# First attention of a fused two-layer kernel: blanks written in pairs from an earlier half on, first batch's totals inverted sooner, maxima products repeated behind the break of a half

## The chip, the cores and the metric

The kernel runs on one NeuronCore of a Trainium2 chip. The metric is the device time of one execution in microseconds. An execution with the hardware profiler on gives the rows that are read here: which engine ran what, when, and at what granted TensorE clock. The engines are called PE (TensorE; PEld is its weight load), DVE (VectorE), ACT (ScalarE), POOL (GpSimd) and SP (SyncE, which here only issues transfers).

## What is computed

Four blocks on a batch of 4 sequences of 1024 tokens with 256 features, each followed by a residual sum and a layer norm: an attention with 16 heads of 16, a feed-forward of width 768, a causal attention with 8 heads, and a feed-forward of 16 experts. The change touches the first attention and its border with the feed-forward. That attention, with the reference's names:

```
q, k = apply_rope(layer_norm(q), layer_norm(k));  q = q * 16 ** -0.5
attn = softmax(einsum('bqhd,bkhd->bhqk', q, k), axis=-1)
out  = einsum('bhqk,bkhd->bqhd', attn, v).reshape(B, S, C)
x    = layernorm(x + out @ w_proj.T + b_proj)
```

## The kernel before

The first attention (`phase_attention0`) works through 16 **groups** of four heads of one batch, four groups to a batch. A group has 64 **units** (one tile of 128 keys, 512 queries, one head each) in two **halves** of 32. So there are 32 halves, counted by `u` from 0 to 31 (`TURNS`). Order on every engine is written out by hand, and the engines meet at semaphores only.

For each unit PE makes a **score** product (`score`, L867) into one of three PSUM banks, and ACT takes its exponential (L935). Score `s` waits for the exponential of three units before. PE goes in **bursts** of three units, and each burst may be followed by **value** products (`values`, L839), whose results lie `LAG` = 6 units and, in the first rounds of a half, up to `BREAK` = 3 more behind the scores. So at the start of each half there is a **break**: from unit 6 to unit 11 of the half no value products run. ACT also copies the finished half out there (`copy_out`, L928).

Softmax needs each query's maximum first. So with each unit PE also makes a **maxima** product (`max_product`, L814) for a unit `AHEAD` = 24 steps (48 units) later, into one of four banks, and DVE reduces it (`take`, L959). At the end of a half's 32 reductions DVE joins them (L968), POOL cuts the result in two parts (`cut_maxima`, L761 and L763), PE turns them (`turn_max`, L826; just before units 23 and 55 of a group, the **turn**), ACT copies them (L922), and SP moves them with four small transfers (`rows`, L695) into the queries' stack, where the first score of the next half waits for them. Both halves of a score or maxima product's pair use different rows of PE's array, so a score and a maxima product can run at the same time.

SP's queue holds, in this order in each group: the store of the last half of the group before (L702), the rows of its own second half, a **stack load** (L537 and L540: twelve transfers of 128 KB and one of 512 KB, for the group three later, up to group 12), the store of its first half, and the rows for the next group.

POOL's queue holds, in half `u`: `cut_maxima(u)`, fetches and preparation of weights (halves 6 to 17), and from half 18 (`FIRST_BLANKS`) five **blanks** a half (L792): transfers of about half a megabyte of zeros each, 32 in all, into two scratch arrays of the expert stage. Each blank waits for the landing of the one before. When all are out, POOL waits for the first tokens of the feed-forward (`xin`) and adds the bias to them (L798).

The exponentials' sums (**totals**) of the first three batches are read back at group 13 (`GROUPS - 3`), inverted by DVE when its last maximum is taken (L977), and written out as `shares` by SP in group 15. Then SP loads sums, shares and tokens of the first two blocks of the feed-forward (L487, L489, L502). The buffers for these are the stacks of groups 12 and 13. The fourth batch's totals are handled in the feed-forward.

Between the stages stands a barrier of all engines (L103). In the feed-forward (`phase_ffn0`) ACT's first function with a table of its own is the square root in `deviation` (L1336).

Of the kernel before, what the change touches and what calls it, by code (L numbers as in the profile page):

```python
# [14 lines left out]
P = 128  # L15
# [527 lines left out]
def phase_attention0(nc, d, keep, weights, stacks, shared):  # L543
# [68 lines left out]
    LAG, BREAK = 6, 3  # L612

# [36 lines left out]
    with ExitStack() as ctx:  # L650
# [28 lines left out]
        EARLY_TOKENS = (BATCH - 1) * SEQ  # L679
        totals = zero[:, 0:EARLY_TOKENS // shared.CUTS]  # L680
# [6 lines left out]
        def _(sp):  # L687
# [19 lines left out]
            for g in range(GROUPS):  # L707
# [9 lines left out]
                if g == GROUPS - 1:  # L717

                    sp.wait_ge(shares_made, 1)
                    sp.dma_start(shared.shares_of(d, slice(0, EARLY_TOKENS)), totals).then_inc(shares_out, 16)  # L720
                    sp.wait_ge(shares_out, 16)
                    sp.wait_ge(pv_done, (GROUPS - 2) * ROUNDS + RING // G0)
                    for n in range(2):
                        shared.load_sums(sp, d, n)
                        shared.load_tokens(sp, d, n)
# [3 lines left out]
                if g == 0:  # L729
                    stacks.load(sp, d, 0, 3)  # L730
                if g == GROUPS - 3:
# [4 lines left out]
                    sp.dma_start(totals, shared.totals_of(d, slice(0, EARLY_TOKENS))).then_inc(totals_in, 16)  # L736
            store(GROUPS - 1, 1)
            for half in range(HALVES):
                sp.wait_ge(out_stored[half], 16 * (GROUPS + 1 - half))

        @block.gpsimd
        def _(pool):
# [25 lines left out]
            FIRST_WEIGHTS, FIRST_BLANKS, BLANKS, LAST_FETCH = 11, 18, 5, 26  # L768

            for u in range(TURNS):  # L770
# [12 lines left out]
                if u >= FIRST_BLANKS:  # L783
                    first = (u - FIRST_BLANKS) * BLANKS
                    for n, (rows, block) in enumerate(blanks[first:first + BLANKS]):

                        if n + first == 0:
                            pool.wait_ge(zeroed, 1)
                        else:
                            pool.wait_ge(zero_out, 16 * (n + first))  # L790
                        out = rows.rearrange("(n p r) c -> n p (r c)", p=P, r=ZERO_ROWS)[block]
                        pool.dma_start(out, zero[:, 0:out.shape[1]]).then_inc(zero_out, 16)  # L792
            assert (TURNS - FIRST_BLANKS) * BLANKS >= len(blanks) == ZERO_DMAS
            pool.wait_ge(zero_out, 16 * ZERO_DMAS)
            pool.wait_ge(shared.bproj_in, 16)
            for n in range(2):
                pool.wait_ge(shared.xin_in[n], 16)
                pool.tensor_tensor(shared.xin[:, n], shared.xin[:, n], shared.bproj[:].unsqueeze(1).to_broadcast([P, TPK, DIM]),  # L798
                                   ALU.add).then_inc(shared.biased, 1)
# [2033 lines left out]
```

## Time and profile before

| | |
|---|---|
| median of 3 runs | 2048.72 us (2048.32 to 2051.12) |
| profiled execution | 2047.03 us, span 2045.1 us |
| mean granted TensorE clock | 0.917 |
| busy in the span | PE 1797.7, PEld 1140.7, DVE 1456.4, ACT 1110.0, POOL 515.3 us |
| DVE L959, reductions of the first attention's maxima | 1024, busy 623.5 us, 50.3 us idle before them |
| ACT L935, most of its exponentials | 1000, busy 524.1 us, 90.0 us idle before them |
| first attention | from about 136 to 831 us of the span |

Times of rows are microseconds from the start of the span. In a timeline each row has its start, its length, the engine, the line of the kernel and the operation, the output and the inputs, how many instructions are merged in it (x), and in brackets the idle time before it with what ended it. "POOLq" or "SPq" marks what the queue of that engine issues. A digit in the page's slices is a share in tenths, 9 being 90% or more.

### The profile page before, as it was taken

The page shows a single profiled execution, that of the slowest core. Times are in us where ns is not written, and L with a number is a line of the kernel's source. Part 1 is how long each engine was busy: PE and PEld are TensorE (multiplying, and loading weights), DVE is VectorE, ACT ScalarE, POOL GpSimd, SP SyncE. Part 2 cuts the span into 40 slices and gives each one's busy share as a digit, 9 for nine tenths or more (in the row PEclk, how much of TensorE's full clock was granted, in tenths as well). Part 3 has the DMA queues.
Part 4 walks back from the last instruction along what each step waited for, and adds up shares of the span by engine and source line. Part 5 has one row for each costly group of instructions (what it writes and reads, how often), then busy time and mean ns, then how long its engine had stood idle before and what let it go on. Part 6 is the DMA issues. An engine that isn't in the chain of part 4 may idle for free. (4 is left out here: it accounts for less than half of the span.)

```text
span 2045.1 us, 34014 instructions
## 1 busy us (share of the span) xinstructions
PE 1797.7 (88%) x12327; PEld 1140.7 (56%) x12327; DVE 1456.4 (71%) x2824; ACT 1110.0 (54%) x2199; POOL 515.3 (25%) x672
## 2 busy tenths in 40 slices
PE   8979999999988999699999879899999629999960
PEld 4544444444433443488888745555555318988960
DVE  7869999999988996467676455566666236666637
ACT  4636888888877888222222225454545314445526
POOL 5740000322111000222321122215151431433323
PEclk9977999999988999799999869999999858999985
DMA  4883635433765301214533455637362305444316
GB/s 174 282 228 48 100 74 110 90 59 61 179 183 166 61 17 45 77 42 137 159 117 114 150 150 115 149 72 184 86 166 60 117 22 198 136 141 147 126 48 221
DMA packets 167745, 245.87 MB, mean 120 GB/s; under 512 B 26078, under 2 KB 101635, under 8 KB 167600
## 3 DMA queue, kind: packets, MB, share of 16 engines
q1 hardware_dynamic: 139744, 178.76, 35.5%
q0 software_dynamic: 11744, 33.75, 4.7%
q10 hardware_dynamic: 16112, 31.46, 4.4%
q8 instruction: 86, 1.41, 0.3%
q14 instruction: 59, 0.48, 0.1%
HBM read 141.10 MB, written 100.66 MB: 118 GB/s over the span
## 5 line engine op out<-in xcount | busy, mean ns | idle before, releaser
L959 DVE TENSOR_REDUCE b_mx<-b_PM 128x1 f32<-128x512 f32 x1024 | 623.5, 681 | 50.3 <-PE b_PM L814 49.8
L935 ACT ACTIVATE b_probs<-b_PS 128x512 f32<-128x512 f32 x1000 | 524.1, 607 | 90.0 <-PE b_PS L867 74.7
L814 PE MATMUL b_PM<-b_kst,b_qst 48*128 48x512 f32 x768 | 276.8, 452 | 0.0
L867 PE MATMUL b_PS<-b_qst,b_kst 50*128 50x512 f32 x744 | 265.3, 449 | 12.6 <-ACT b_probs L935 12.5
L2305 ACT ACTIVATE d_probs<-d_PS 128x512 f32<-128x512 f32 (+3 forms) x384 | 166.5, 497 | 187.5 <-PE d_PS L2218 186.9
L2343 DVE TENSOR_REDUCE d_mx<-d_PM 128x2 f32<-128x1024 f32 (+1 forms) x192 | 180.2, 951 | 110.8 <-PE d_PM L2170 63.3
L867 PEld LDWEIGHTS b_PS<-b_qst,b_kst 50*128 50x128 f32 x744 | 123.7, 189 | 187.0 <-ACT b_probs L935 171.0
L839 PE MATMUL b_PO<-b_probs,b_vst 128*32 128x384 f32 (+3 forms) x1960 | 150.7, 415 | 1.0 <-ACT b_probs L935 0.9
L839 PE MATMUL b_PO<-b_probs,x_v 128*32 128x384 f32 (+2 forms) x2048 | 148.9, 398 | 0.0
L2268 POOL TENSOR_SCALAR_AFFINE_SELECT d_probs<-d_probs 128x128 f32<-128x128 f32 x256 | 77.4, 315 | 267.6 <-ACT d_probs L2305 263.2
L2546 ACT ACTIVATE f_h<-f_PH,w_b 128x512 f32<-128x512 f32 x96 | 66.2, 689 | 140.5 <-PE f_PH L2505 130.3
L814 PEld LDWEIGHTS b_PM<-b_kst,b_qst 48*128 48x128 f32 x768 | 128.3, 189 | 3.4
L2650 DVE TENSOR_TENSOR f_h_low<-f_h,f_h_high 128x512 fp32r<-128x512 f32 x96 | 66.5, 693 | 79.2 <-ACT f_h_high L2548 79.2
L761 POOL CAST b_mhalves<-b_maxima 128x16 fp32r<-128x16 f32 x32 | 6.3, 197 | 449.0 <-DVE b_maxima L968 433.7
L1218 POOL TENSOR_TENSOR c_hT<-c_hidden,c_hT 128x512 fp32r<-128x512 f32 x48 | 64.7, 1347 | 212.8 <-DVE c_hT L1456 212.8
L2559 POOL DMA_INDIRECT answers<-f_y,f_to x48 | 82.7, 1724 | 137.2 <-issue 87.0
L2218 PE MATMUL d_PS<-d_qst,d_kst 98*128 98x512 f32 (+3 forms) x288 | 106.7, 387 | 8.0 <-ACT d_probs L2305 4.8
L814 PE MATMUL b_PM<-x_k,x_q 48*128 48x512 f32 x256 | 107.4, 537 | 7.0 <-DVEq L951 6.7
L2520 PE MATMUL f_PY<-f_w_high,f_h_high 128*128 128x256 f32 x384 | 108.9, 284 | 0.0
L2505 PE MATMUL f_PH<-f_xT,f_w_high 128*128 128x512 f32 x384 | 107.0, 401 | 1.4 <-DVE f_xT L2638 1.4
L2520 PE MATMUL f_PY<-f_w_low,f_h_high 128*128 128x256 f32 x384 | 107.9, 281 | 0.0
L2520 PE MATMUL f_PY<-f_w_high,f_h_low 128*128 128x256 f32 x384 | 107.9, 281 | 0.0
(279 smaller groups left out, 3587.3 us busy)
## 6 DMA issues: line engine op xcount, KB each, us to landing
halves<-a_parts SPq DMA_DIRECT2D x7, 2048.0 KB
qk<-c_halves ACTq DMA_DIRECT2D x7, 2048.0 KB, 12.4
w_w<-L_ffn_fc1T SPq DMA_DIRECT2D x12, 1024.0 KB, 4.8
w_w<-L_ffn_fc2T SPq DMA_DIRECT2D x12, 1024.0 KB, 5.4
b_qst<-halves SPq DMA_DIRECT2D x72, 128.0 KB, 4.8
b_kst<-halves SPq DMA_DIRECT2D x72, 128.0 KB, 7.5
d_qst<-qk SPq DMA_DIRECT2D x36, 256.0 KB, 4.5
d_kst<-qk SPq DMA_DIRECT2D x36, 256.0 KB, 6.6
```

What stands on the lines that cost most here:

```text
L814: pe.matmul(PM[n % MBANKS][:], qst[buf][at, p, first:first + P], kst[buf][at, p, kh * BLK:(kh + 1) * BLK], start=True, stop=True).then_inc ...
L839: mm = pe.matmul(PO[j * VS0:(j + 1) * VS0, cols], vst[g % BUFS][:, kt, j, :], probs[:, (R * G0 + i) % RING, cols], start=(kt == 0 and firs ...
L867: pe.matmul(score_bank(g, s)[:], kst[g % BUFS][at, p, kt * P:(kt + 1) * P], qst[g % BUFS][at, p, half * BLK:(half + 1) * BLK], start=True, ...
L935: act.activation(probs[:, s % RING], score_bank(g, s)[:], ACT.Exp).then_inc(exped, 1)
L959: dve.tensor_reduce(mx[:, half, (r * PAIRS0 + p) * TPH + t, kh:kh + 1], PM[n % MBANKS][:], AX.X, ALU.max)\
L2218: pe.matmul(PS[bank(s)][:, 0:w], kst[g % BUFS][0:KM, j, kt * P:(kt + 1) * P], qst[g % BUFS][0:KM, j, q0:q0 + w], start=True, stop=True).th ...
L2268: pool.affine_select(out=near, in_=near, pattern=[[1, P]], compare_op=ALU.is_ge, fill=0.0, base=0, channel_multiplier=-1)\
L2305: act.activation(probs[:, s % RING, 0:w], PS[bank(s)][:, 0:w], ACT.Exp).then_inc(exped, 1)
L2343: dve.tensor_reduce(mx[:, :, qt, kh], PM[n][:, :, 0:keys(qt, kh)], AX.X, ALU.max).then_inc(max_taken[n], 1)
L2505: mm = pe.matmul(PH[f % 4][:], w[:, c, at], xT[:, half, c, :], start=(k == 0 and c == 0), stop=(k == 2 and c == CD - 1))
L2520: mm = pe.matmul(PY[t % 2][:], hidden[:, f, at], w[:, i, f, :], start=(f == 0 and k == 0), stop=(f == FC - 1 and k == 2))
L2559: pool.indirect_dma_start(out=d["answers"], out_offset=bass.IndirectOffsetOnAxis(ap=index.bitcast(U32), axis=0), in_=src, in_offset=None, ...
```

## The change

Five edits:

- PE repeats maxima products: that of unit 7 of each half is made three times, those of units 8, 9 and 10 twice, with the same operands into the same bank. Only the last counts up the semaphore. The last half of the last group has no maxima products and so no repeats.
- POOL issues the blanks two a half, in halves 9 to 24, in place of five a half from 18 on. The pair waits for the pair of the half before and for this half's rows to have landed, and not for each other.
- Totals of the first batch are read back in group 4, into a buffer of their own, inverted by DVE between the maxima of group 6, and written out in group 7. Those of the second and third batch take the way of before, and their shares are written out at the end of SP's group 15.
- SP loads sums, shares and tokens of the first two blocks in group 14, not in group 15, since they are all of the first batch. POOL adds the bias to the tokens in half 30.
- ACT computes a square root of one column as the first thing of the feed-forward, into a buffer that nothing reads.

```diff
+    REPEATS = {7: 3, 8: 2, 9: 2, 10: 2}
...
+        first_totals = a.sb("first_totals", [P, SEQ // shared.CUTS])
+        totals = zero[:, 0:(BATCH - 2) * SEQ // shared.CUTS]
+        TOTALS_GROUP = HG0 + 3
...
-                if g == GROUPS - 1:
-
-                    sp.wait_ge(shares_made, 1)
-                    sp.dma_start(shared.shares_of(d, slice(0, EARLY_TOKENS)), totals).then_inc(shares_out, 16)
+                if g == GROUPS - 2:
+
                     sp.wait_ge(shares_out, 16)
-                    sp.wait_ge(pv_done, (GROUPS - 2) * ROUNDS + RING // G0)
+                    sp.wait_ge(pv_done, g * ROUNDS + RING // G0)
                     for n in range(2):
                         shared.load_sums(sp, d, n)
                         shared.load_tokens(sp, d, n)
...
+                if g == HG0:
+
+                    for half in range(HALVES):
+                        sp.wait_ge(out_stored[half], 16 * (HG0 + 1))
+                    sp.dma_start(first_totals[:], shared.totals_of(d, FIRST_TOKENS)).then_inc(totals_in, 16)
+                if g == TOTALS_GROUP:
+                    sp.wait_ge(shares_made, 1)
+                    sp.dma_start(shared.shares_of(d, FIRST_TOKENS), first_totals[:]).then_inc(shares_out, 16)
                 if g == GROUPS - 3:
...
-                    sp.dma_start(totals, shared.totals_of(d, slice(0, EARLY_TOKENS))).then_inc(totals_in, 16)
+                    sp.dma_start(totals, shared.totals_of(d, MORE_TOKENS)).then_inc(totals_in, 16)
+                if g == GROUPS - 1:
+                    sp.wait_ge(shares_made, 2)
+                    sp.dma_start(shared.shares_of(d, MORE_TOKENS), totals).then_inc(shares_out, 16)
...
+            sp.wait_ge(shares_out, 32)
...
-            FIRST_WEIGHTS, FIRST_BLANKS, BLANKS, LAST_FETCH = 11, 18, 5, 26
+            FIRST_WEIGHTS, FIRST_BLANKS, BLANKS, LAST_FETCH = 11, 9, 2, 26
...
-                if u >= FIRST_BLANKS:
-                    first = (u - FIRST_BLANKS) * BLANKS
-                    for n, (rows, block) in enumerate(blanks[first:first + BLANKS]):
-
-                        if n + first == 0:
-                            pool.wait_ge(zeroed, 1)
-                        else:
-                            pool.wait_ge(zero_out, 16 * (n + first))
+                first = (u - FIRST_BLANKS) * BLANKS
+                if 0 <= first < len(blanks):
+
+                    if first == 0:
+                        pool.wait_ge(zeroed, 1)
+                    else:
+                        pool.wait_ge(zero_out, 16 * first)
+                    pool.wait_ge(rows_in, (u + 1) * ROW_DMAS)
+                    for rows, block in blanks[first:first + BLANKS]:
                         out = rows.rearrange("(n p r) c -> n p (r c)", p=P, r=ZERO_ROWS)[block]
                         pool.dma_start(out, zero[:, 0:out.shape[1]]).then_inc(zero_out, 16)
+                if u == TURNS - 2:
+
+                    pool.wait_ge(shared.bproj_in, 16)
+                    for n in range(2):
+                        pool.wait_ge(shared.xin_in[n], 16)
+                        pool.tensor_tensor(shared.xin[:, n], shared.xin[:, n],
+                                           shared.bproj[:].unsqueeze(1).to_broadcast([P, TPK, DIM]), ALU.add)\
+                            .then_inc(shared.biased, 1)
...
-            pool.wait_ge(shared.bproj_in, 16)
-            for n in range(2):
-                pool.wait_ge(shared.xin_in[n], 16)
...
-            def max_product(g, x, kh):
+            def max_product(g, x, kh, times=1):
...
-                pe.matmul(PM[n % MBANKS][:], qst[buf][at, p, first:first + P],
-                          kst[buf][at, p, kh * BLK:(kh + 1) * BLK], start=True, stop=True).then_inc(max_scores, 1)
+                for _ in range(times):
+                    mm = pe.matmul(PM[n % MBANKS][:], qst[buf][at, p, first:first + P],
+                                   kst[buf][at, p, kh * BLK:(kh + 1) * BLK], start=True, stop=True)
+                mm.then_inc(max_scores, 1)
...
-                    max_product(ahead, x, s % HALVES)
+                    max_product(ahead, x, s % HALVES, REPEATS.get(s % (UNITS // HALVES), 1))
...
+                if n == HALVES * (TOTALS_GROUP - 1) * HALF_MAXIMA:
+                    dve.wait_ge(totals_in, 16)
+                    dve.reciprocal(first_totals[:], first_totals[:]).then_inc(shares_made, 1)
             join_maxima(TURNS - 1)
-            dve.wait_ge(totals_in, 16)
+            dve.wait_ge(totals_in, 32)
...
-        eps = a.sb("eps", [P, 1])
+        eps, warm = a.sb("eps", [P, 1]), a.sb("warm", [P, 1])
...
             act.wait_ge(prep, 1)
+            act.activation(warm[:], eps[:], ACT.Sqrt)
```

## Rows read from the trace of the kernel before

**Rows 1.** The page, the span in 40 slices of 51.1 us
```profile
DVE  7869999999988996467676455566666236666637
PEclk9977999999988999799999869999999858999985
```

**Rows 2.** Timeline of VectorE, first attention: start us, us
```profile
182.22 12.64 DVE L959 TENSOR_REDUCE b_mx<-b_PM 128x1 f32<-128x512 f32 x21 [0.21 <-PE b_PM L814]
...
783.41 15.04 DVE L959 TENSOR_REDUCE b_mx<-b_PM 128x1 f32<-128x512 f32 x25 [0.21 <-PE b_PM L814]
```

**Rows 3.** Windows: bounds, length, busy us (x) of PE, PEld, DVE, ACT, POOL, clock, DMA
```profile
263.91:285.08 21.17, 20.63 (x195) 9.01 (x195) 19.61 (x33) 17.37 (x35) 0.42 (x2) 0.92 0.75 114
386.39:406.05 19.66, 19.11 (x195) 8.48 (x195) 19.43 (x33) 17.36 (x35) 12.39 (x14) 1.00 0.77 123
584.64:633.19 48.55, 43.01 (x388) 18.46 (x388) 39.30 (x67) 34.98 (x69) 6.38 (x15) 0.86 0.61 175
633.19:680.55 47.36, 41.70 (x388) 17.98 (x388) 39.17 (x67) 34.98 (x69) 3.92 (x10) 0.89 0.48 124
```

**Rows 4.** Windows of one microsecond behind the break of three halves
```profile
193.00:194.00 1.00, 1.00 (x6) 0.28 (x10) 1.00 (x3) 1.00 (x3) 0.00 (x0) 0.55 0.89 119
275.00:276.00 1.00, 1.00 (x10) 0.20 (x8) 1.00 (x3) 1.00 (x3) 0.00 (x0) 0.51 1.04 131
773.00:774.00 1.00, 1.00 (x10) 0.28 (x10) 1.00 (x3) 1.00 (x3) 0.00 (x0) 0.68 0.00 0
```

**Rows 5.** Timeline of PE and ScalarE in the break of a clean half
```profile
391.23 0.62 PE L814 MATMUL b_PM<-b_kst,b_qst 48*128 48x512 f32 x2
...
394.65 0.39 PE L814 MATMUL b_PM<-b_kst,b_qst 48*128 48x512 f32 x1
...
394.94 3.53 ACT L935 ACTIVATE b_probs<-b_PS 128x512 f32<-128x512 f32 x7
...
395.59 0.50 PE L867 MATMUL b_PS<-b_qst,b_kst 50*128 50x512 f32 x1 [0.55 <-ACT b_probs L935]
```

**Rows 6.** Timeline around a late cut of the maxima
```profile
654.89 0.53 POOL L792 DMA_DIRECT2D answers<-b_zero  x1 [9.41 <-DMA answers<-b_zero]
...
656.08 0.44 PE L826 MATMUL b_PS<-const,b_mhalves 128*128 128x128 f32 x1 [4.57 <-POOL b_mhalves L763]
...
658.33 1.89 DVE L959 TENSOR_REDUCE b_mx<-b_PM 128x1 f32<-128x512 f32 x3 [5.70 <-PE b_PM L814]
```

**Rows 7.** Timeline, blanks beside a stack load, then the next rows
```profile
561.68 0.53 POOL L792 DMA_DIRECT2D slots<-b_zero  x1 [8.35 <-DMA slots<-b_zero]
...
564.56 2.58 SPq L695 DMA_DIRECT2D b_qst<-b_mrows  x4
...
567.66 0.50 PE L867 MATMUL b_PS<-b_qst,b_kst 50*128 50x512 f32 x1
...
569.53 0.47 PE L867 MATMUL b_PS<-b_qst,b_kst 50*128 50x512 f32 x1
```

**Rows 8.** Timeline from the first attention into the first feed-forward
```profile
807.90 0.65 SPq L487 DMA_DIRECT2D x_sums<-att  x1
...
815.66 10.23 SPq L702 DMA_DIRECT2D att<-x_outT  x2
...
824.93 0.60 ACT L928 ACTIVATE x_outT<-b_PO 128x512 f32<-128x512 f32 x1 [1.19 <-PE b_PO L839]
...
828.33 2.34 POOL L798 TENSOR_TENSOR x_xin<-x_xin,x_bproj 128x1024 f32<-128x1024 f32 x1 [4.62 <-DMA x_xin<-x]
...
836.08 0.10 POOL L1196 MEMSET c_eps<- 128x1 f32 x1 [5.42 <-POOLq L103]
...
844.34 1.28 ACT L1336 ACT_TABLE_LOAD   x1 [18.82 <-DVE c_moments L1411]
```

**Rows 9.** Timeline of VectorE, break of the first half
```profile
174.05 1.89 DVE L959 TENSOR_REDUCE b_mx<-b_PM 128x1 f32<-128x512 f32 x3 [0.69 <-PE b_PM L814]
```

**Rows 10.** Timeline of VectorE, a reciprocal of 128x128
```profile
851.99 0.94 DVE L1436 RECIPROCAL c_totals<-c_totals 128x128 f32<-128x128 f32 x1
```

More of the change, by code:

```diff
@@ L678, in phase_attention0 @@
         zeroed, zero_out = a.sem("zeroed"), a.sem("zero_out")
-        EARLY_TOKENS = (BATCH - 1) * SEQ
-        totals = zero[:, 0:EARLY_TOKENS // shared.CUTS]
+        FIRST_TOKENS, MORE_TOKENS = slice(0, SEQ), slice(SEQ, (BATCH - 1) * SEQ)
+        first_totals = a.sb("first_totals", [P, SEQ // shared.CUTS])
+        totals = zero[:, 0:(BATCH - 2) * SEQ // shared.CUTS]
+        TOTALS_GROUP = HG0 + 3
         ZERO_DMAS = (E * CAP + TOKENS * TOP_K) // (P * ZERO_ROWS)
@@ L782, in _ @@
                     pool.dma_start(shared.bproj[:], row.to_broadcast([P, DIM])).then_inc(shared.bproj_in, 16)
-                if u >= FIRST_BLANKS:
-                    first = (u - FIRST_BLANKS) * BLANKS
-                    for n, (rows, block) in enumerate(blanks[first:first + BLANKS]):
-                        if n + first == 0:
-                            pool.wait_ge(zeroed, 1)
-                        else:
-                            pool.wait_ge(zero_out, 16 * (n + first))
+                first = (u - FIRST_BLANKS) * BLANKS
[6 more added lines that the diff above has]
+                    for rows, block in blanks[first:first + BLANKS]:
                         out = rows.rearrange("(n p r) c -> n p (r c)", p=P, r=ZERO_ROWS)[block]
                         pool.dma_start(out, zero[:, 0:out.shape[1]]).then_inc(zero_out, 16)
+                if u == TURNS - 2:
[5 more added lines that the diff above has]
+                            .then_inc(shared.biased, 1)
             assert (TURNS - FIRST_BLANKS) * BLANKS >= len(blanks) == ZERO_DMAS
             pool.wait_ge(zero_out, 16 * ZERO_DMAS)
-            pool.wait_ge(shared.bproj_in, 16)
-            for n in range(2):
-                pool.wait_ge(shared.xin_in[n], 16)
-                pool.tensor_tensor(shared.xin[:, n], shared.xin[:, n], shared.bproj[:].unsqueeze(1).to_broadcast([P, TPK, DIM]),
-                                   ALU.add).then_inc(shared.biased, 1)
             pool.wait_ge(shared.biased, 2)
```

## The prediction

> **What bounds the kernel now.** I read the page's slices first, then the edited stage by VectorE's timeline, because VectorE is its fullest engine. In slices 4 to 15 (153 to 767 us, most of the first attention) VectorE stands at 9 except in slices 12 and 13, where the granted clock too is below 9 [rows 1]. A digit does not say who leads, so I looked at a half (32 maxima reductions on VectorE) by its bounds: the reduction that follows VectorE's short idle at each turn of a half. A clean half takes 19.66 us with VectorE busy for 19.43, PE for 19.11 and the clock at 1.00 [rows 3]. So two chains run nearly level: VectorE with 0.23 us to spare, and the loop PE to ScalarE to PE, on whose product that idle ends.
>
> From the idle that ends at 182.22 to that at 783.41 [rows 2] are 601.2 us and 29 halves. Clean, they would take 29 x 19.66 = 570.1. The excess of 31.0 us is what can be won there, and it has two kinds.
>
> First, clock dips. The half from 263.91 takes 21.17 us, 1.51 more than a clean one, at a mean clock of 0.92 [rows 3]. The clock falls to its lower level (1.2 of 2.4 GHz) in the microsecond from 275, just when the break of the half ends [rows 4]: the stretch in which score and maxima products run but no value products. Nine halves carry such a dip, the first in that span from 193, the last from 773 [rows 4].
>
> Second, blanks. From 584.64, two halves take 48.55 us and the next two 47.36, so 9.2 and 8.0 above clean [rows 3]. GpSimd sends five blanks a half, each behind a wait for the one before. One such wait lasts 9.41 us until 654.89, the maxima that are cut behind it are late, PE's turn idles 4.57 us for them, and VectorE then idles 5.70 [rows 6]. Two dips lie in these four halves. At 1.5 us each they are 3.0 of the 17.3, so blanks cost 14.3 and all dips 16.7.
>
> Behind the stage, ScalarE ends at 825.53 and SP has issued the last store at 825.89, yet GpSimd adds the bias until 830.67, because its tokens landed only at 828.33. The next stage's first instruction is at 836.08, 5.41 after GpSimd [rows 8].
>
> **The change, part by part.**
>
> *Repeats.* Five maxima products more in each of 31 halves (the last has none): two extra for unit 7 of the half, one extra for units 8, 9 and 10. A second product in one burst adds 0.23 us (0.62 for two, 0.39 for one) [rows 5]. What hides them: between units 7 (394.65) and 8 (395.59) PE has 0.94 us, of which it idles 0.55, and three products need 0.39 + 2 x 0.23 = 0.85. From unit 8 on, one unit starts each 0.49 us, since ScalarE runs seven exponentials in 3.53 us without a gap ((3.53 - 0.60) / 6), and two products issue in about 2 x 0.23 = 0.46 [rows 5]. Should a score be late all the same, ScalarE has cover: unit 8's score is there at 396.09 and its exponential, the fourth of the seven, starts near 394.94 + 3 x 0.49 = 396.41, so 0.32 us. VectorE sees unit 8's maxima at 396.09 + 0.23 = 396.32. It takes them as the 18th reduction after the turn, at 386.39 + 17 x 0.60 = 396.59 (21 take 12.64) [rows 2, 3], so it isn't starved either. Nothing, therefore, at the high clock. Without that cover it is 5 x 0.23 = 1.15 us a half. What they bring: PE is filled exactly in the stretch after which the clock falls. The trace of before cannot show that the clock then holds. Its bounds are none of 16.7 and all of it. I take all, because in the dense stretches of the same halves the clock stands at 1.00 and under a third of the halves dip at all, so the fault is a near miss.
>
> In the first half the clock is low already and the loop PE-bound: VectorE waits 0.69 us for it at 174.05 [rows 9]. There the repeats are on the path, at twice the price: 5 x 0.46 = 2.3 at most, nothing at least (the clock may rise sooner). I take 2.0, near the top.
>
> *Blanks.* Two a half from the tenth half, then 16 halves long, issued once this half's row transfers have landed, and behind a wait for the pair of the half before. That pair is then a whole half old (19.66 us, against 9.41 for the slowest landing shown), so the wait is nothing. The new wait for the rows delays only the two issues behind it; the next cut is due a half later. All 14.3 comes back. Late next is the clean loop, at 19.66.
>
> Both kinds of DMA meet in the odd halves, where SP loads a stack. The nearest row is a half with about three blanks beside a stack load: one took over 8 us to land, rows were issued at 564.56, and the score that needs them started at 569.53, where the 1.69 us pitch of the bursts (567.66 before it) puts 569.35 [rows 7]. That is 0.18 us. Eight such halves: 1.4, with 0 below and 1 us each, 8, above.
>
> The Trainium skill, "DMA: Bandwidth & Descriptors", section "Issuing engines are not separate DMA queues", speaks against this move: transfers of all issuing engines run on the same 16 DMA engines and interleave. By it a blank is never free beside a stack load, only moved to other halves; the rows bear it out in the landing of 8.35 us, and it would give the third rival below.
>
> *Totals.* A reciprocal of 128x128 is put between VectorE's maxima. Such a one takes 0.94 us [rows 10]; the halves give back 0.23 each. Between nothing and 0.94 I take 0.5. The final one shrinks, off the path. SP's extra small transfers lie behind the rows, with nothing urgent queued.
>
> *Loads of sums and tokens, a group sooner.* In their old place they span 807.90 to 828.33, 20.4 us [rows 8]. In the new one they begin some 3 us after the rows of a turn, so their tail lies over the next rows on the same queue, 19.66 later: between nothing and 3 us, once. I take 1.0. The bias on GpSimd (2 x 2.3 [rows 8]) follows them, about 13 us behind its cut, ahead of the next one.
>
> *Exit.* Without the bias the stage ends with SP at 825.89, so 830.67 - 825.89 = 4.8 comes back. If the barrier's 5.41 didn't follow the last engine, it would be nothing.
>
> *Warm Sqrt.* The table load of 1.28 us starts at 844.34, when the moments are there [rows 8], and PE's next transposes hang on it. It moves into ScalarE's idle: 1.3. The Trainium skill, "ScalarE: Activation LUTs", section "What ACT_TABLE_LOAD costs", counts a drain with each switch, 2.66 us in all; by that the gain would be 1.4 larger. The trace shows the load alone, and it decides.
>
> **The sum.** Won: 31.0 + 4.8 + 1.3 = 37.1. Paid: 2.0 + 1.4 + 0.5 + 1.0 = 4.9. Net 32.2. The profiled execution took 2047.03 (1.9 around its span of 2045.1), so 2014.8. The median of the runs is 2048.72, 1.7 above it: 2016.5. I round to 2016.
>
> **Rivals.**
>
> *The repeats don't hold the clock.* For it: pairs of products kept PE going before too, and the clock fell. Against: they ran at 0.49 us for what issues in 0.23. Price 16.7: about 2033; with half of the dips, 2024. Chance 0.16.
>
> *The repeats land on the path.* For it: PE shows 19.11 of 19.66 busy, and the covers are hundredths to tenths. If every repeat were exposed, 31 x 1.15 = 36 us would go, 2052 with the rest as summed; with the larger of the other bounds (6.6 for rows, 2 for loads) 2061, slower than before. It decides from 0.9 of the repeats exposed. Against: the idle of 0.55 and ScalarE's 0.32. A third exposed gives 2028. Chance 0.06, of which 0.02 for full exposure.
>
> *Blanks and stack loads hold the rows back.* Up to 8 us in those halves and 3 in the load's: 2025. For it: the 8.35 us. Against: 0.18 us of harm then. Chance 0.10.
>
> *More than I count.* The first half pays nothing, the halves run below 19.66, later stages gain: 2011. Chance 0.06.
>
> Mine, 2012 to 2021: 0.62.
>
> **Range.** From 2010, below the better case, to 2032, which takes in half-kept dips and most of the full ones, the partial exposure and the rows: about 0.87. Less than 0.2% (4.1 us, what a measurement of this kernel can tell from no change) could come out only of the repeats' full exposure: faster 0.97, same 0.01, slower 0.02.
>
> **What would show it.** Right: VectorE's halves at 19.66 throughout, no microsecond with the clock at 0.50 behind a break, units 8 to 11 still 0.49 apart on PE; the turn fed without idle from 584 to 680; blanks from about 345 on; from ScalarE's last copy to the next stage some 6 us; no table load before the first deviation. Wrong: breaks with the clock still at 0.50 (the first rival), clean-clock halves longer than 19.7 (the second), scores of a half's first unit waiting for rows in halves 10 to 25 (the third).

## The result, and the profile after

The changed kernel takes 2005.11 us, median of four runs (2001.05 to 2007.55), against 2049.92 for the kernel before in the same comparison: ratio 0.9777, 95% interval 0.9756 to 0.9799. A second comparison, on another chip, gave 2004.41 and 0.9802 (0.9771 to 0.9832). I had forecast 2016, in a range from 2010 to 2032. The sign was right, the size too small by about a quarter, and the range's near end lies above what was measured.

The page of the changed kernel, its slices of 50.1 us, beside [rows 1]:

```profile
DVE  7869999999999994677676455665655337666637
...
PEclk9977999999999999899999779999999759999985
```

Slices 12 and 13 are full now. Next its timeline of VectorE; the first two rows lie in the break of the first half and answer to [rows 9], the reductions behind an idle of about 0.2 us are turns of a half, as in [rows 2], and the reciprocal is the one that was added:

```profile
174.52 1.89 DVE L980 TENSOR_REDUCE b_mx<-b_PM 128x1 f32<-128x512 f32 x3 [1.25 <-PE b_PM L834]
...
177.96 1.29 DVE L980 TENSOR_REDUCE b_mx<-b_PM 128x1 f32<-128x512 f32 x2 [1.55 <-PE b_PM L834]
...
183.41 15.65 DVE L980 TENSOR_REDUCE b_mx<-b_PM 128x1 f32<-128x512 f32 x26 [0.22 <-PE b_PM L834]
...
360.35 15.64 DVE L980 TENSOR_REDUCE b_mx<-b_PM 128x1 f32<-128x512 f32 x26 [0.21 <-PE b_PM L834]
...
376.00 0.94 DVE L998 RECIPROCAL b_first_totals<-b_first_totals 128x128 f32<-128x128 f32 x1
...
400.05 5.47 DVE L980 TENSOR_REDUCE b_mx<-b_PM 128x1 f32<-128x512 f32 x9 [0.22 <-PE b_PM L834]
```

The last short idle of the 29 halves ends at 753.86. From 183.41 that is 570.45 us, 19.67 a half, where before it was 601.2 [rows 2]. No microsecond between 185 and 798 has a granted clock below 0.90. The two halves around the reciprocal take 39.70 us, 0.36 more than two others.

The break of a half on PE, which answers to [rows 5]:

```profile
388.65 0.85 PE L834 MATMUL b_PM<-b_kst,b_qst 48*128 48x512 f32 x3
389.59 0.50 PE L888 MATMUL b_PS<-b_qst,b_kst 50*128 50x512 f32 x1
389.59 0.73 PE L834 MATMUL b_PM<-b_kst,b_qst 48*128 48x512 f32 x2
390.08 0.49 PE L888 MATMUL b_PS<-b_qst,b_kst 50*128 50x512 f32 x1
...
391.06 0.50 PE L888 MATMUL b_PS<-b_qst,b_kst 50*128 50x512 f32 x1
```

Three maxima products stand for unit 7, and PE reaches unit 8's score after 0.94 us as before, without the idle of 0.55. From 389.59 to 391.06 the scores are 0.49 apart. The extra products lie where nothing waits for them.

The exit, which answers to [rows 8], in the timeline of all engines:

```profile
736.77 0.64 SPq L487 DMA_DIRECT2D x_sums<-att  x1
...
756.71 2.38 POOL L812 TENSOR_TENSOR x_xin<-x_xin,x_bproj 128x1024 f32<-128x1024 f32 x1 [3.88 <-DMA x_xin<-x]
...
795.43 0.60 ACT L949 ACTIVATE x_outT<-b_PO 128x512 f32<-128x512 f32 x1 [1.19 <-PE b_PO L860]
...
796.05 0.33 SPq L705 DMA_DIRECT2D att<-x_outT  x1
...
797.97 0.10 POOL L1220 MEMSET c_eps<- 128x1 f32 x1 [28.28 <-POOLq L103]
...
798.19 1.28 ACT L1356 ACT_TABLE_LOAD   x1 [2.16 <-PEq L103]
...
798.53 4.64 PE L1261 MATMUL c_PO<-u_w_proj,x_att2T 128*128 128x256 f32 x24 [3.17 <-DVEq L1426]
...
807.48 1.97 PE L1254 MATMUL c_PG<-const,c_x 128*128 128x128 f32 x8 [4.31 <-DVE c_x L1443]
```

The next stage's first instruction comes 1.94 us after ScalarE's last copy ended, and 1.59 after SP issued the last store.

Where the 39.3 us of the two profiled executions lie, stage by stage, and what I had forecast:

| stretch, us | before | after | won | forecast |
|---|---|---|---|---|
| to ScalarE's last copy | 824.93 | 795.43 | 29.5 | 26.1 |
| from there to the next stage | 11.15 | 2.54 | 8.6 | 4.8 |
| feed-forward | 349.9 | 344.1 | 5.8 | 1.3 |
| second attention and routing | 499.6 | 504.7 | -5.0 | 0 |
| the rest | 359.5 | 359.1 | 0.4 | 0 |
| span | 2045.1 | 2005.8 | 39.3 | 32.2 |

The boundaries are first instructions: [rows 8] and the one at 797.97 for the feed-forward, and for the second attention this cast, in the kernel before and then in the changed one:

```profile
1185.96 1.73 DVE L2332 CAST d_fixed<-const 128x128 bf16<-128x128 f32 x2 [7.73 <-PEq L103]
```
```profile
1142.06 1.73 DVE L2357 CAST d_fixed<-const 128x128 bf16<-128x128 f32 x2 [7.66 <-PEq L103]
```

Two theories about the first stretch had to be told apart: that clock and blanks cost their own parts, as I had split them, or that they cost partly the same time. Three more questions came from the table: the exit, the feed-forward, and the loss behind it.

### The profile page after: what moved, and what is told of

Read it like the earlier page. It is cut to its first block and busy times, and to the rows that moved or that the text cites. A ratio compares the mean times of both kernels' runs of the same rounds, so it can differ in the third digit from the quotient of the medians.

```text
span 2005.8 us, 34345 instructions
## 1 busy us (share of the span) xinstructions
PE 1790.2 (89%) x12482; PEld 1155.4 (58%) x12482; DVE 1451.1 (72%) x2825; ACT 1110.1 (55%) x2200; POOL 514.6 (26%) x672
## 3 DMA queue, kind: packets, MB, share of 16 engines
q1 hardware_dynamic: 140032, 178.76, 35.4%
## 5 line engine op out<-in xcount | busy, mean ns | idle before, releaser
L834 PE MATMUL b_PM<-b_kst,b_qst 48*128 48x512 f32 x888 | 281.5, 431 | 0.0
L888 PE MATMUL b_PS<-b_qst,b_kst 50*128 50x512 f32 x744 | 257.2, 437 | 1.8
L834 PEld LDWEIGHTS b_PM<-b_kst,b_qst 48*128 48x128 f32 x888 | 142.1, 185 | 5.1
L860 PE MATMUL b_PO<-b_probs,b_vst 128*32 128x384 f32 (+3 forms) x1960 | 143.0, 397 | 1.0 <-ACT b_probs L956 0.9
```

The costliest lines, as they stand in the source:

```text
L834: mm = pe.matmul(PM[n % MBANKS][:], qst[buf][at, p, first:first + P], kst[buf][at, p, kh * BLK:(kh + 1) * BLK], start=True, stop=True)
L860: mm = pe.matmul(PO[j * VS0:(j + 1) * VS0, cols], vst[g % BUFS][:, kt, j, :], probs[:, (R * G0 + i) % RING, cols], start=(kt == 0 and firs ...
L888: pe.matmul(score_bank(g, s)[:], kst[g % BUFS][at, p, kt * P:(kt + 1) * P], qst[g % BUFS][at, p, half * BLK:(half + 1) * BLK], start=True, ...
```

## The experiments

Ratios are to the kernel before in the same comparison. "Copy" is the start of ScalarE's last copy, 824.93 before and 795.43 after. From one copy of a finished half to the next (L928 before, L949 after) a clean half takes 19.66 us; where a half's length is given below, it is that distance. There are 30 breaks with maxima products in them, from the second half to the 31st.

### Without the repeats

```diff
-    REPEATS = {7: 3, 8: 2, 9: 2, 10: 2}
+    REPEATS = {}
```

> The changed kernel without the repeated maxima products. Theory (the repeats hold the clock): the clock stands at 0.50 again behind the breaks of some 7 to 12 of the 31 halves, 1.5 us or more each, and the first half gains back about 1.2 us; the time is 12 to 18 us above the changed kernel, so about 2018 to 2024 (ratio to before 0.985 to 0.988). Rival (the dips went because blanks and loads lie elsewhere, not because of the repeats): the halves stay at 19.66, and the time is about 1 us below the changed kernel, ratio about 0.977.

2021.34 us (2016.76 to 2025.99), ratio 0.9877 (0.9851 to 0.9902). Copy at 805.11. Seven dips are back. One of them in windows of a microsecond, and the timeline of PE and VectorE at the same place:

```profile
432.00:433.00 1.00, 1.00 (x8) 0.46 (x12) 1.00 (x3) 1.00 (x3) 0.00 (x0) 0.99 1.03 391
433.00:434.00 1.00, 1.00 (x8) 0.02 (x3) 1.00 (x3) 0.85 (x2) 0.00 (x0) 0.50 1.19 254
```
```profile
430.97 0.49 PE L888 MATMUL b_PS<-b_qst,b_kst 50*128 50x512 f32 x1 [0.55 <-ACT b_probs L956]
...
435.11 1.89 DVE L980 TENSOR_REDUCE b_mx<-b_PM 128x1 f32<-128x512 f32 x3 [0.70 <-PE b_PM L834]
437.64 1.29 DVE L980 TENSOR_REDUCE b_mx<-b_PM 128x1 f32<-128x512 f32 x2 [0.64 <-PE b_PM L834]
```

The clock falls to its lower level right behind a break in which PE's longest idle is 0.55 us. These two idles of VectorE are 1.34 us, and a half with such a fall takes 21.16 to 21.19 us, 1.5 more than a clean one. The repeats hold the clock. With everything else changed they are worth 9.7 us of the first stretch (805.11 - 795.43): 10.6 in the seven halves, less 0.9 by which the first half ended sooner without them. The medians lie 16 us apart, the two profiled executions 9.

### The blanks as before

```diff
-            FIRST_WEIGHTS, FIRST_BLANKS, BLANKS, LAST_FETCH = 11, 9, 2, 26
+            FIRST_WEIGHTS, FIRST_BLANKS, BLANKS, LAST_FETCH = 11, 18, 5, 26
```

and each blank waits for the one before it again.

> The changed kernel with the blanks as before: five a half from half 18, each behind the landing of the one before. Theory: POOL's cut comes late in two halves as before, each with about 6 us of idle on VectorE, and the low clock after them; together 12 to 15 us more than the changed kernel, so 2017 to 2020. Rival (the stalls of before came of the low clock and the blanks only kept it company): with the clock held, a late cut costs nothing or a few us, total under 2010.

2014.94 us (2013.45 to 2016.51), ratio 0.9843 (0.9819 to 0.9866). Copy at 800.73. GpSimd, PE and VectorE around the only late cut, which answers to [rows 6]:

```profile
595.34 0.53 POOL L805 DMA_DIRECT2D answers<-b_zero  x1 [2.89 <-DMA answers<-b_zero]
595.86 0.21 POOL L774 CAST b_mhalves<-b_maxima 128x16 fp32r<-128x16 f32 x1
...
596.52 0.44 PE L846 MATMUL b_PS<-const,b_mhalves 128*128 128x128 f32 x1 [3.62 <-POOL b_mhalves L776]
...
598.77 1.89 DVE L979 TENSOR_REDUCE b_mx<-b_PM 128x1 f32<-128x512 f32 x3 [4.75 <-PE b_PM L833]
```

One cut was late, where the kernel before loses 17.3 us in four halves [rows 3]. So the old blanks cost only 5.3 us (800.73 - 795.43), not 14.3, when the clock holds. The late half itself takes 26.15, 6.5 more than a clean one; another 1.2 went to a wait for rows (see "The changed kernel once more"), and the first half happened to end 2.4 sooner. The time lies between the two theories.

### The old totals, loads, bias and table

The kernel before with the repeats and the new blanks alone.

> The kernel before with the repeats and the new place of the blanks alone; totals, loads of sums and tokens, the bias and the square root are as before. Theory: first attention as in the changed kernel, but from ScalarE's last copy to the first instruction of the next stage 10.6 us again (5.4 of it behind POOL's last addition) and the table load back: 10 us more than the changed kernel (8.6 at the border, 2.0 behind it, small change), 2013 to 2017. Rival (only the 4.8 us of bias and the 1.3 of the table come back, the rest of the surplus lies elsewhere): 6 us more, 2011.

2019.86 us (2011.53 to 2023.20), ratio 0.9860 (0.9831 to 0.9888). Copy at 795.75, as in the changed kernel. GpSimd's timeline at the exit:

```profile
799.41 2.34 POOL L800 TENSOR_TENSOR x_xin<-x_xin,x_bproj 128x1024 f32<-128x1024 f32 x1 [4.32 <-DMA x_xin<-x]
807.16 0.10 POOL L1200 MEMSET c_eps<- 128x1 f32 x1 [5.42 <-POOLq L103]
```

The two edits inside the halves bring 29.2 us of the first stretch; totals and earlier loads neither help nor harm it in these two profiles. The next stage begins 9.2 us later than with the changed border, and the feed-forward takes 350.6. The time is 3 us above the theory's range.

### The extra products elsewhere in the half

```diff
-    REPEATS = {7: 3, 8: 2, 9: 2, 10: 2}
+    REPEATS = {14: 3, 15: 2, 16: 2, 17: 2}
```

> The changed kernel with the same five extra products a half, but at units 14 to 17, where value products run too. Theory (what counts is that the break is filled): dips come back as without repeats, and the extra products lie on PE's path, 0.6 to 1.15 us in every half: halves of 20.2 to 20.8 us, total 2030 to 2050. Rival (any extra product work anywhere in a half holds the clock): no dips, and only the path cost, 2022 to 2035 with a clock of 1.00 in every microsecond behind a break.

2043.58 us in the one run. Between 185 and 794 the clock doesn't dip, though the break is as empty as before, so it held behind 29 of the 30 breaks. Behind the thirtieth it fell, and stayed low until 808. PE in that break, and two windows of a microsecond:

```profile
792.16 0.50 PE L888 MATMUL b_PS<-b_qst,b_kst 50*128 50x512 f32 x1 [0.54 <-ACT b_probs L956]
```
```profile
793.00:794.00 1.00, 1.00 (x6) 0.37 (x4) 1.00 (x3) 1.00 (x4) 0.00 (x0) 1.00 0.21 76
794.00:795.00 1.00, 1.00 (x10) 0.16 (x8) 1.00 (x3) 1.00 (x3) 0.00 (x0) 0.69 0.00 0
```

VectorE's timeline, the same place of two successive halves:

```profile
407.11 1.29 DVE L980 TENSOR_REDUCE b_mx<-b_PM 128x1 f32<-128x512 f32 x2 [0.58 <-PE b_PM L834]
...
427.70 1.29 DVE L980 TENSOR_REDUCE b_mx<-b_PM 128x1 f32<-128x512 f32 x2 [0.59 <-PE b_PM L834]
```

A half takes 20.58 us instead of 19.67, and the last copy starts at 830.85. Of the 35.4 us to the changed kernel's 795.43, 26.2 lie in 29 halves, 0.91 each, 6.3 behind the fall at 794, and 2.9 in the first half. So the place decides what the products cost, 0.9 us a half where PE is full and nothing in the break. My idea that the clock falls unless the break itself is filled does not hold: 29 breaks went without a fall, where the kernel without repeats has 7 falls in 30. But one fall is left here, and the profiles with products in the break have none behind a break. One execution can't tell whether the two places are equally good. Half length and time are in the theory's range, the clock is nearly the rival's.

### The repeats alone

The kernel before with the repeats.

> The kernel before with the repeated products alone. The blanks (five a half from turn 18, chained), the totals, the loads at the end and the square root's table stay as they were. Theory A (the clock and the blanks each cost their own part): the repeats remove the clock's dips, 16.7 us by the prediction's split of the 31.0 us, and cost the first half 1.2 us; the blanks' stalls of 14.3 us stay. 15 to 16 us won, ratio about 0.992. Theory B (most of what looked like the blanks' stall was the slow clock that goes with it): with the old blanks in the changed kernel only 6.8 us of vector idleness were left over beside the 6.2 of the changed kernel itself, so the repeats alone win 35.2 - 13.0 - 1.2 = 21 us, ratio about 0.990. In the trace both expect no low-clock microsecond between 185 and 590, and one stall of some 5 us at a blank's row wait near 600; B expects the sum of vector idle time before turn reductions after 182 us at 13 us, A at 18 to 20.

2026.80 us (2021.42 to 2031.15), ratio 0.9904 (0.9874 to 0.9934). Copy at 801.14; no low clock between 185 and 598; one late cut, VectorE's largest idle in the 31 halves:

```profile
600.15 1.89 DVE L962 TENSOR_REDUCE b_mx<-b_PM 128x1 f32<-128x512 f32 x3 [4.01 <-PE b_PM L816]
```

VectorE's idle before turn and break reductions after 182 sums to 12.99 us, theory B's 13. The whole time is 18.5 us under the kernel before, between the two theories, and the first stretch 23.8. The copies then give both prices from both sides:

| to the last copy, us won | other edit absent | other edit there |
|---|---|---|
| repeats | 23.8 (alone) | 9.7 |
| new blanks | 19.8 (without repeats) | 5.4 |
| both | 29.2 | |

(The 19.8 has the changed border with it, worth 0.3.) The two overlap by 14 us. How early the first half ends differs by up to 2.8 us between profiles with the same repeats in it. Counted without it, over the next 29 halves alone, the four numbers are 24.4, 10.6, 20.1 and 6.4, both together 30.7, and the overlap is again 14. It sits mostly in one place: the kernel before has two late halves of 27.36 and 27.71 us, and with the repeats alone the same two take 24.72 and 20.59. My split of 16.7 and 14.3 described neither edit.

### The bias last on GpSimd

```diff
+            pool.wait_ge(exped, GROUPS * UNITS + SBANKS)
             for n in range(2):
                 pool.wait_ge(shared.xin_in[n], 16)
```

and the additions stand behind this wait, at the end of GpSimd's queue.

> The changed kernel with GpSimd's two additions of the bias (2.38 us each) held back until ScalarE's last exponential is through, so that GpSimd ends the stage as it did before. Theory A (what follows the stage comes 5.4 us after GpSimd's last instruction, and under 2 us after any other engine's): additions at about 796, end near 801, the next stage's first instruction near 806.5 instead of 798.0; the time rises by 7 to 9 us, ratio to the kernel before about 0.981. Theory B (the step to the next stage takes the same after the last engine, whichever it is, and the 5.4 us before belonged to stores still under way): the next stage begins 1.6 to 2 us after the second addition, near 803; the time rises by some 5 us.

2013.53 us (2009.51 to 2021.54), ratio 0.9837 (0.9801 to 0.9873). GpSimd's timeline:

```profile
803.23 4.64 POOL L813 TENSOR_TENSOR x_xin<-x_xin,x_bproj 128x1024 f32<-128x1024 f32 x2 [26.62 <-ACT b_probs L955]
813.29 0.10 POOL L1219 MEMSET c_eps<- 128x1 f32 x1 [5.42 <-POOLq L103]
```

The additions end at 807.87, and 5.42 us follow, where the changed kernel shows 1.94 after ScalarE. ScalarE's last copy had ended at 804.79, 3.1 us before GpSimd. Theory A. The whole kernel's time can't be laid on this alone, since this profile also shows a low clock from 762 to 780, which put the copy at 804.19. It follows no plain break: PE had stood still for 1.80 us before the first score of that half.

```profile
760.57 0.47 PE L887 MATMUL b_PS<-b_qst,b_kst 50*128 50x512 f32 x1 [1.80 <-issue]
```

### One tile that nothing uses

```diff
-        eps = a.sb("eps", [P, 1])
+        eps, warm = a.sb("eps", [P, 1]), a.sb("warm", [P, 1])
```

in the feed-forward of the kernel before, nothing else.

> The kernel before with one more tile of one float a partition allotted behind eps in the feed-forward stage and never used, which moves every later tile of that stage in SBUF and changes no instruction. Theory A (the feed-forward stage of the changed kernel took 344.1 us against 349.9, and the attention after it 504.6 against 499.6, because its tiles lie elsewhere): this kernel shows about 346 and 504.6, and its time stays within 2 us of the kernel before. Theory B (these two differences come from the changed code or from when the clock falls and rises at a stage's end): both stages stay at 350 and 499.6, time unchanged.

2041.64 us (2028.12 to 2047.59, ten runs), ratio 0.9974 (0.9950 to 0.9997). The feed-forward takes 344.7 us instead of 349.9, with the same instructions. The down projection's products in groups by line, in the kernel before, in this one, and in the changed one:

```profile
L1237 PE MATMUL c_PO<-u_w_down,c_hT 128*128 128x256 f32 x576 | 71.8, 283 | 0.6 <-DVE c_s L1462 0.6
```
```profile
L1237 PE MATMUL c_PO<-u_w_down,c_hT 128*128 128x256 f32 x576 | 69.3, 279 | 0.6 <-DVE c_s L1462 0.6
```
```profile
L1261 PE MATMUL c_PO<-u_w_down,c_hT 128*128 128x256 f32 x576 | 69.6, 279 | 0.6 <-DVE c_s L1487 0.6
```

Theory A for the feed-forward: of its 5.2 us, 2.5 are in these products and 2.2 in those of the gate and up projections (77.6 to 76.6 and 75.6 to 74.4 us busy). For the attention behind it this run showed 505.6 us, which also fitted theory A; the repetition below weakens that.

### The first half without repeats

```diff
-                    max_product(ahead, x, s % HALVES, REPEATS.get(s % (UNITS // HALVES), 1))
+                    max_product(ahead, x, s % HALVES, REPEATS.get(s % (UNITS // HALVES), 1) if HALVES * g + 2 * s // UNITS else 1)
```

> The changed kernel with the maxima products of the first half, whose clock is at 0.50 anyway, issued once each; from the second half on they are repeated as in the change. Theory A (the repeats lie on the path while the clock is low): the first half's products are 5 fewer at 0.43 us each, the idle times of VectorE at 174.5 and 178.0 (1.25 and 1.55 us) shrink to those before, the first turn reduction of the steady halves is back at 182.2 from 183.4, the time falls by 1.2 us. Theory B (the repeats bring the clock up earlier, or hold it in the first warm half): the reduction at 182 comes no earlier and a low stretch appears between 185 and 200, the time is the same or up to 1.5 us longer. Ratio to the kernel before 0.977.

2001.98 us (1999.43 to 2008.12), ratio 0.9789 (0.9760 to 0.9818): no difference from the changed kernel that can be told. VectorE's timeline in the first half:

```profile
173.92 1.89 DVE L980 TENSOR_REDUCE b_mx<-b_PM 128x1 f32<-128x512 f32 x3 [0.69 <-PE b_PM L834]
177.36 1.29 DVE L980 TENSOR_REDUCE b_mx<-b_PM 128x1 f32<-128x512 f32 x2 [1.55 <-PE b_PM L834]
```

The first idle is back at the 0.69 us of [rows 9], the second stays, and the turn's reduction comes at 182.69 instead of 183.41. The copy starts at 795.69 all the same. Theory A in mechanism, 0.7 us in size, and lost again later: one half takes 19.93 and one 20.34.

### The changed kernel once more

> The changed kernel itself once more, for comparisons on one chip: ratio to the kernel before 0.978 +- 0.002, stages 798, 344, 504.6, 303, 56 us in its profile.

2004.41 us (2002.91 to 2012.11), ratio 0.9802. Copy at 795.41, feed-forward 343.7, second attention and routing 501.1. In the same kernel that last stage took 504.7 the first time. The windows from 395 us into it, of the first profile and then of this one (they reach 5 and 9 us into the stage behind it):

```profile
1537.10:1652.10 115.00, 55.32 (x214) 33.38 (x214) 38.12 (x190) 30.61 (x63) 38.78 (x56) 0.66 0.24 75
```
```profile
1536.60:1651.60 115.00, 52.98 (x224) 33.29 (x221) 42.77 (x196) 32.56 (x65) 38.73 (x56) 0.69 0.27 86
```

The mean clock there is 0.66 and 0.69. Over the whole stage the clock is low in 12 stretches, 132 us together, in the first profile, and in 8 of 120 us in this one. How many it has differs from one execution of the same instructions to the next, and its length with it.

In the first attention, one half differs too. The first score of a half waits for its rows, and behind the loads of sums and tokens it came late here:

```profile
758.45 0.46 PE L888 MATMUL b_PS<-b_qst,b_kst 50*128 50x512 f32 x1 [0.90 <-issue]
```

That half takes 20.57 us, against 19.68 in the first profile. In five of the ten profiles with the moved loads PE stands still there for 0.61 to 1.80 us, and the half is 0.7 to 3.1 us longer; in the other five, and in the four with the loads in their old place, it isn't. The trace names no releaser, so that the rows landed late beside the loads is inferred from the wait in the kernel.

### The tiles where they lay before

```diff
-        eps, warm = a.sb("eps", [P, 1]), a.sb("warm", [P, 1])
+        eps = a.sb("eps", [P, 1])
...
         vaug = a.sb("vaug", [P, 2, TPK, H1, VS1])
+        warm = a.sb("warm", [P, 1])
```

in the changed kernel.

> The changed kernel with the tile that the square root's early table load writes to allotted last in the feed-forward stage instead of second, so that the stage's other tiles lie where they lay before the change; no instruction changes. Theory A (the tiles' places are worth the 5 us by which the timed runs won more than the profiled one, as one unused tile alone gave a ratio of 0.9974): ratio to the kernel before 0.980, 4 to 6 us over the changed kernel; the feed-forward stage at 349 to 350 less 2.0 = 348, c_PO's products of the down projection 283 ns apiece instead of 279. Theory B (the unused tile's 0.9974 was the spread of the runs): the same time as the changed kernel, within 2 us, whatever the stage shows.

2007.90 us (2004.73 to 2009.23), ratio 0.9808 (0.9779 to 0.9836). Feed-forward 347.8 us, 4 more than in the same comparison's changed kernel, and the products are back at their old duration:

```profile
L1262 PE MATMUL c_PO<-u_w_down,c_hT 128*128 128x256 f32 x576 | 71.8, 283 | 0.6 <-DVE c_s L1488 0.6
```

The medians differ by 3.5 us in the expected direction, the ratios by less than their intervals. The trace decides for theory A in the stage; the whole time alone would not have told it.

### One repeat a half

```diff
-    REPEATS = {7: 3, 8: 2, 9: 2, 10: 2}
+    REPEATS = {7: 2}
```

> The changed kernel with one repeat a half (unit 7 twice) instead of five (7 three times, 8, 9 and 10 twice). Theory A (what counts is that TensorE isn't idle at the one place behind the break; one more product of 0.39 us isn't enough of the 1.6 us idle there): several of the seven dips that the kernel without repeats shows stay, time between that kernel's and the change's, ratio about 0.983. Theory B (any extra work at the break holds the clock, as a few extra products elsewhere did too): no low-clock microsecond between 185 and 790, time as the change's, ratio 0.978. Theory C (all or nothing at five): seven dips as without repeats, ratio 0.988.

2012.49 us (2010.26 to 2014.22), ratio 0.9834 (0.9797 to 0.9871). Copy at 794.11, and no low clock between 185 and 790: theory B, in the one profile there is. The windows from 185 to 590 of the kernel without repeats, of this one, and of the changed one:

```profile
185.00:590.00 405.00, 394.10 (x3914) 173.40 (x3908) 393.97 (x668) 352.17 (x688) 63.95 (x96) 0.98 0.51 113
```
```profile
185.00:590.00 405.00, 398.46 (x3989) 177.54 (x3987) 400.63 (x681) 358.85 (x701) 64.03 (x96) 1.00 0.54 119
```
```profile
185.00:590.00 405.00, 403.32 (x4073) 188.40 (x4073) 400.66 (x681) 359.01 (x701) 63.88 (x96) 1.00 0.54 118
```

VectorE does the same work in the same time with one extra product a half as with five. Yet the kernel took some 8 us longer than the changed one, of which its profile shows 7.4 in the second attention and routing (508.1 against 501.1 and 504.7). Nothing there depends on the edit that I can name. This stays open.

### Without the early table load

```diff
-            act.activation(warm[:], eps[:], ACT.Sqrt)
```

in the feed-forward; the tile stays.

> The changed kernel without ScalarE's early square root at the start of the feed-forward stage; its tile stays allotted. Theory A (the early load takes the table's 1.28 us off the path and nothing else): the span from the stage's first instruction to TensorE's first transposes grows from 9.51 to 10.8 us (11.54 before, the rest being TensorE's clock, still 1.00 at the stage's start), time up by 1.3 us. Theory B (all of the 2.03 us is the table's): it grows to 11.5, time up by 2 us. Either is within what the timed runs can tell from nothing, so the trace decides.

2005.63 us (2002.82 to 2006.80), ratio 0.9793 (0.9756 to 0.9830). The timelines of ScalarE and PE:

```profile
804.33 1.28 ACT L1360 ACT_TABLE_LOAD   x1 [10.37 <-DVE c_moments L1435]
805.62 0.30 ACT L1360 ACTIVATE c_std<-c_moments,c_eps 128x4 f32<-128x4 f32 x1
```
```profile
796.46 5.48 PE L1261 MATMUL c_PO<-u_w_proj,x_att2T 128*128 128x256 f32 x24 [3.17 <-DVEq L1425]
```

From the stage's first instruction (795.90) to PE's transposes (807.61) are 11.7 us, against 9.5. Of the 2.2 the table is 1.28, and 0.84 is that the first 24 products take 5.48 us instead of 4.64: the clock was at 0.50 from 795 here, behind the same 3.17 us of idle after which it was 1.00 until 799 in the changed kernel. So the 2.03 us that the changed kernel won at this place are 1.3 from the edit, and the rest is when the clock fell.

## Why the prediction was right or wrong, point by point

- **What can be won in the halves, 31.0 us.** Right: 601.19 became 570.45, 30.7.
- **Its split, 16.7 for dips and 14.3 for blanks.** Wrong as prices of the edits. Each alone brings far more (23.8 and 19.8), each beside the other far less (9.7 and 5.4). I divided four halves by subtracting two dips at 1.5 us each, though two of the nine, from 193 and from 691, cost 3.0 each. But the halves with late blanks were also those with the longest low clocks: in or right behind each stall of VectorE and PE the clock fell, and with the clock held the second late half shrank from 27.71 to 20.59. That a low clock leaves less cover for the next cut would explain this; it isn't shown by itself. The sum survived only since both edits were made together.
- **Repeats hidden.** Right, in the place that I computed: scores 0.49 apart, PE's 0.55 of idle gone. The run with the same five products elsewhere shows the other case at 0.91 us a half; I had put it at 1.15.
- **Repeats hold the clock.** Right; the reason, that PE must be filled in exactly that stretch, was too narrow. One product in the break does it, and five in a full part of the half did it behind 29 of 30 breaks. A rule of the Trainium skill stands behind these rows: "TensorE: Matmul & The Clock Gate", section "What's actually happening", calls the low clock the default, which activity lifts. The trace agrees in that with the same idle of 0.55 us in the break, the falls go from 7 to 1 in 30 when PE is given five more products elsewhere.
- **The first half, 2.0.** 1.2 in the profile; without its repeats 0.7 came back there. In the run with unmoved tiles, the same first attention had its clock at 1.00 by 175 and its copy at 794.22. ScalarE's first copy, in the second half, starts between 188.98 and 191.81 in the nine profiles with repeats in the first half's break, and between 190.24 and 190.76 in the four without. The term is of the size of one execution's luck.
- **Rows beside blanks and stack loads, 1.4, and the earlier loads, 1.0.** Both nothing in this profile: 29 halves at 19.67. For the blanks that holds in every profile, within 0.3 us. Behind the loads PE paused in five of ten profiles, 0.61 to 1.80 us, inside my bounds of nothing and 3, so their nothing here is luck. **Reciprocal, 0.5:** 0.36. Of 4.9 us booked for costs 1.6 were paid in this profile.
- **Exit, 4.8.** This step failed: it measured 8.6. I let the 5.41 us follow whichever engine is last. They follow GpSimd; after ScalarE 1.94 follow. Of the 3.8 that I missed, 3.5 is this difference. I had read one exit, with GpSimd last, and gave the other possibility only a lower value, nothing, never a higher one.
- **Table, 1.3.** Right, 1.28. The drain that the Trainium skill ("ScalarE: Activation LUTs", "What ACT_TABLE_LOAD costs") adds doesn't show: in the last experiment the square root starts 1.29 us after the load did.
- **A term that I left out.** The new tile behind `eps` moves all later tiles of the feed-forward, and its products run 283 to 279 ns. 3.8 us of the stage (5.8 less the 2.0 at its start), confirmed in both directions: 5.2 us less when the tile was added to the kernel before, 4.1 more when it was moved out of the changed one's way.
- **Behind it.** -5.0 in the first profile, -1.4 in the second, with the same instructions. I had taken everything behind the feed-forward's start as equal between two executions. It swings by several us. It may not be chance alone: the stage takes 499.6 to 503.2 us in the four profiles with the feed-forward's tiles in their old place, and 501.1 to 508.1 in the ten with moved ones, eight of them between 504.5 and 505.6. No experiment says why, and this stays open.

Together: 3.4 in the first attention, 3.8 at the exit, 4.5 in the feed-forward, less 4.6 behind, are the 7.1 us between 32.2 and 39.3. The timed runs lie lower still: I had added 1.7 to go from the profiled execution to the median, and here the profiled one, 2007.55, is the highest of its four, 2.4 above it. These 4.1 us are the spread of the runs and no step of the kernel. My case "more than I count" named two of these sources and went to 2011 at 0.06. Its low end should have held the refund of all booked costs (4.9) and some gain of each unmeasured boundary.

## What to carry to other kernels

Price two edits that touch the same stall both alone and together before naming a share for either, since a stall and the slow clock behind it are partly one cost. If TensorE's clock dips in breaks of a loop, try one repeated product where the engine idles anyway; elsewhere the same product costs its time. When a stage's end is shortened, ask which engine is last and what follows that engine, and when a tile is added anywhere, compare the durations of instructions that nobody edited.

## What the runs showed of the hardware

- After the last instruction of a stage, the next stage's first came 5.42 us later when GpSimd's addition of the bias was last (before, and in four experiments) and 1.94 us after ScalarE's last copy when GpSimd had long been done. Other last instructions of GpSimd weren't tried.
- An unused tile of one float a partition changed fp32 products of 128x256 from 283 to 279 ns and a stage from 349.9 to 344.7 us. Moving it behind the other tiles brought 283 ns back. Which address matters wasn't tried.
- The granted clock fell to its lower level behind a break with no idle above 0.55 us, in 7 to 9 of 30 breaks, in one of 30 with five more products elsewhere in the half, and never there in the ten profiles with one or five more products in the break.
- The same instructions gave a second attention and routing of 501.1 and 504.7 us, and the same 3.17 us of idle left the clock at 1.00 in one execution and at 0.50 in another.
